# A recurrent two-layer block on one core: negated row maxima transposed twelve columns at a time and sent as one transfer, a turn without TensorE's self-wait, GpSimd's second remainders after the first maxima

## What is computed

```python
    Q, K, V = (heads(WQ), heads(WK), heads(WV))
    score = jnp.einsum('bhqd,bhkd->bhqk', Q, K) / jnp.sqrt(jnp.asarray(D_K, x.dtype))
    score = score + mask
    score = score - jnp.max(score, axis=-1, keepdims=True)
    score = jnp.exp(score)
    score = score / jnp.sum(score, axis=-1, keepdims=True)
    out = jnp.einsum('bhqk,bhkd->bhqd', score, V)
```

```python
    xn = _layernorm(x, axis=-1)
    s = _L0_attn_ref(xn, ...)
    g = _silu(_L0_ffn_ref(xn, ...))
    x = x + s * g
```

## Time and profile before

| | us |
|---|---|
| median of 3 runs | 636.89 (636.42 to 638.6) |
| the profiled execution: its span | 632.9 |
| its own time as a run | not given; the median is 4.0 above the span |
| PE busy | 580.1 (92%) |
| DVE busy | 486.8 (77%) |
| ACT busy | 327.5 (52%) |
| GpSimd busy | 177.4 (28%) |
| chain that ended last | PE 71%, DVE 17%, ACT 3%, issue 3% |

### The profile page before, as it was taken

The page is one execution under the profiler, slowest core; times in us unless marked ns, Lnnn a source line. Parts: engine busy times, 40 slices in busy tenths (PEclk is TensorE's granted clock), DMA queues, the critical chain, the costliest instruction groups (busy, mean ns, idle before and its releaser), DMA issues.

```text
span 632.9 us, 12434 instructions
## 1 busy us (share of the span) xinstructions
PE 580.1 (92%) x4195; PEld 362.5 (57%) x4222; DVE 486.8 (77%) x1174; ACT 327.5 (52%) x587; POOL 177.4 (28%) x162
## 2 busy tenths in 40 slices
PE   2877999999999999899999988888989999999996
PEld 1434544444444445699999963435436666566554
DVE  6789989999989898555555578765779899976465
ACT  2842467575767667555555558664141652263224
POOL 2450000000134342033333320000005687588500
PEclk9888899999999999999999999998799999999999
DMA  7935726060714080221111124205000322331232
GB/s 190 252 119 200 240 69 209 2 207 4 189 53 108 32 239 19 46 53 46 46 50 46 30 79 140 69 14 171 0 13 34 72 66 74 92 110 41 75 100 66
DMA packets 55755, 58.00 MB, mean 92 GB/s; under 512 B 8794, under 2 KB 39546, under 8 KB 55658
## 3 DMA queue, kind: packets, MB, share of 16 engines
q1 hardware_dynamic: 51386, 50.56, 28.4%
q0 software_dynamic: 4320, 6.81, 3.4%
HBM read 41.96 MB, written 18.85 MB: 96 GB/s over the span
## 4 chain that ended last, share of the span: by engine, by line
PE 71%; DVE 17%; ACT 3%; issue 3%; DMA 1%; POOL 1%; SPq 1%; another core or an unknown queue 0%; DVEq 0%; ACTq 0%; PEldq 0%; POOLq 0%
PE banks L1635 11%; PE banks L1780 8%; PE banks L1723 7%; PE banks L1701 7%; PE banks L1912 7%; PE banks L1647 6%; PE banks L1901 5%; PE banks L1898 4%; PE banks L1963 4%; DVE banks L1185 3%; DVE mpart L1188 2%; PE banks L1595 2%; PE banks L1704 2%; ACT arena L754 1%; POOL rows_a L572 1%
## 5 line engine op out<-in xcount | busy, mean ns | idle before, releaser
L754 ACT ACTIVATE arena<-banks 128x512 f32<-128x512 f32 (+1 forms) x304 | 156.3, 585 | 95.5 <-PE banks L1704 53.8
L1723 PE MATMUL banks<-arena 96*128 96x512 bf16 (+3 forms) x384 | 118.3, 339 | 6.0 <-DVE mpart L1185 2.1
L1701 PE MATMUL banks<-arena 128*128 128x512 bf16 (+3 forms) x358 | 106.1, 326 | 5.8 <-ACT arena L754 3.0
L1188 DVE TENSOR_REDUCE mpart<-banks 128x1 f32<-128x512 f32 x128 | 86.1, 685 | 9.4 <-PE banks L1723 8.8
L1185 DVE CUSTOM_DVE_ANT_0 banks<-banks,arena 128x512 f32<-128x512 f32 (+1 forms) x128 | 79.1, 636 | 8.2 <-PE banks L1723 5.3
L1635 PE MATMUL banks<-arena 128*128 128x128 f32 x624 | 76.3, 275 | 1.0 <-ACT arena L695 1.0
L1635 PEld LDWEIGHTS banks<-arena 128*128 128x128 f32 x624 | 72.8, 192 | 1.5 <-ACT arena L695 1.5
L1780 PE MATMUL banks<-arena 128*9 128x512 f32 (+3 forms) x768 | 70.7, 487 | 0.0
L1701 PEld LDWEIGHTS banks<-arena 128*128 128x128 bf16 x384 | 37.8, 99 | 52.3 <-issue 25.6
L797 ACT ACTIVATE arena<-banks 125x512 f32<-125x512 f32 (+2 forms) x48 | 28.5, 595 | 71.3 <-PE banks L1898 46.3
L601 POOL DMA_INDIRECT results<-arena x39 | 37.5, 961 | 88.5 <-DVE arena L1079 88.5
(11 more groups left out here) (293 smaller groups left out, 909.8 us busy)
## 6 DMA issues: line engine op xcount, KB each, us to landing
k_parts<-arena SPq DMA_DIRECT2D x6, 768.0 KB, 7.6
arena<-in_L_ffn_experts_w_dram SPq DMA_DIRECT2D x2, 2048.0 KB, 10.5
arena<-results SPq DMA_DIRECT2D x8, 512.0 KB, 7.3
arena<-k_parts SPq DMA_DIRECT2D x7, 576.0 KB
arena<-q_parts SPq DMA_DIRECT2D x28, 144.0 KB
arena<-in_L_ffn_w_kernel_dram SPq DMA_DIRECT2D x8, 344.0 KB
slots<-in_pad_rows_dram SPq DMA_DIRECT2D x1, 2535.0 KB, 12.2
arena<-slots SPq DMA_DIRECT2D x39, 65.0 KB, 1.9
```

Source lines behind the costliest of these rows:

```text
L754: act.activation(Pr[:, r % 4, heads[0]:heads[-1] + 1, 0:n], ring_e[e % 3][:, 0:len(heads) * n].rearrange("p (j c) -> p j c", j=len(heads)) ...
L1188: ins = dve.tensor_reduce(part, ps[:, 0:n], AX_X, ALU.max)
L1701: ins = pe.matmul(ring_e[e % 3][:, at * n:at * n + n], QK[:, slot, j, 1, P * kt:P * kt + P], QK[:, slot, j, 0, q:q + n], start=True, stop= ...
L1723: ins = pe.matmul(ps[:, at * n:at * n + n], QK[0:TALL, slot, j, 0, P * i:P * i + P], QK[0:TALL, slot, j, 1, 512 * half:512 * half + n], st ...
```

## The change

Three things.

1. MP becomes [slot, 8 tiles, 12 columns], column a x 4 + j for part a of head j, without a memset. A maxima row is four matmuls (one a tile) of 12 stationary columns into partitions 0 to 11; DVE copies only those 12 partitions; SP sends them in one transfer. DVE no longer waits for its own copy nor counts m_free for a maxima row: PE, when it wants that bank again, waits for mrow_ready instead. Tables worked out from PLANS (ring_tables) say which semaphore and value frees each unit.
2. The last transpose of a turn adds to m_ready itself; PE doesn't wait for it. The semaphore turned goes, and ACT waits for m_ready in its place.
3. GpSimd's second pair of remainders (s = 2 and 3) waits for mp_ready, the first negated maxima.

```diff
+def ring_tables():
+    frees, unit_of, reads_before, reads = [], {}, {}, 0
+    for k in range(-1, NG + 1):
+        for step in PLANS[k]:
+            if step[0] in RING_STEPS:
+                unit_of[step] = len(frees)
+            if step[0] == "maxrow":
+                frees.append(("mrow_ready", 2 * step[1] + step[2] + 1))
+            elif step[0] in RING_STEPS:
+                reads += 1
+                frees.append(("m_free", reads))
+            elif step[0] in ("negmax", "experts0"):
+                reads_before[step] = reads
+    return frees, unit_of, reads_before, reads
...
-        MP = region(24832, 1024, BF16).rearrange("p (s m c) -> p s m c", s=2, m=32)
+        MP = region(24832, 2 * QT * 3 * HG // 2, BF16).rearrange("p (s i c) -> p s i c", s=2, i=QT)
...
-                    for j in range(HG):
-                        sp.dma_start(QK[TALL:TALL + 3, g % 3, j, 0, 512 * half:512 * half + 512],
-                                     mrow[32 * j:32 * j + 3, g % 2, 512 * half:512 * half + 512]).then_inc(mrow_in[half], 16)
+                    sp.dma_start(QK[TALL:TALL + 3, g % 3, :, 0, 512 * half:512 * half + 512],
+                                 mrow[0:3 * HG, g % 2, 512 * half:512 * half + 512]).then_inc(mrow_in[half], 16)
...
-            pool.memset(MP, 0.0).then_inc(Z["mem_set"], 1)
...
             for s in (0, 2):
+                if s == 2:
+                    pool.wait_ge(Z["mp_ready"], 1)
                 second_part(s)
...
                         if g >= 1:
-                            act.wait_ge(Z["turned"], 2 * (g - 1) + half + 1)
+                            act.wait_ge(Z["m_ready"], UNIT_OF[("turn", g - 1, half)] + 1)
...
-                        mp = MP[:, g % 2, :, :].rearrange("p (j i) c -> p j i c", j=HG)[:, :, tiles, :]
+                        mp = MP[:, g % 2, tiles, :].rearrange("p i (a j) -> p j i a", j=HG)
...
-                            dve.wait_ge(mrow_in[half], 64 * (g - 1))
-                        dve.tensor_copy(mrow[:, g % 2, 512 * half:512 * half + 512], ps).then_inc(Z["mrow_ready"], 1)
-                        dve.wait_ge(Z["mrow_ready"], 2 * g + half + 1)
-                        dve.sem_inc(Z["m_free"], 1)
+                            dve.wait_ge(mrow_in[half], 16 * (g - 1))
+                        dve.tensor_copy(mrow[0:3 * HG, g % 2, 512 * half:512 * half + 512], ps[0:3 * HG, :]).then_inc(Z["mrow_ready"], 1)
...
             def unit_free():
                 if unit >= 4:
-                    pe.wait_ge(Z["m_free"], unit - 3)
+                    name, n = FREES[unit - 4]
+                    pe.wait_ge(Z[name], n)
...
                         for i in range(4):
-                            for j in range(HG):
-                                ins = pe.matmul(ps[32 * j:32 * j + 32, P * i:P * i + P],
-                                                MP[:, g % 2, j * QT + 4 * half + i, :], ident_b, start=True, stop=True)
+                            ins = pe.matmul(ps[0:3 * HG, P * i:P * i + P], MP[:, g % 2, 4 * half + i, :], ident_b, start=True, stop=True)
...
-                        ins.then_inc(Z["turned"], 1)
-                        pe.wait_ge(Z["turned"], 2 * g + half + 1)
-                        pe.sem_inc(Z["m_ready"], 1)
+                        ins.then_inc(Z["m_ready"], 1)
```

More of the change, by code:

```diff
@@ L210 @@
 PLANS = all_plans()
+RING_STEPS = ("p1", "logits", "counts", "maxrow", "turn", "attn_turn", "attn_out", "x_turn", "places1", "logits1")
+def ring_tables():
[12 more added lines that the diff above has]
+    return frees, unit_of, reads_before, reads
+FREES, UNIT_OF, READS_BEFORE, READS = ring_tables()
 def build(nc, x, WQ, WK, WV, WO, gate, w1, w2, w3, WomT, b_om, log_scale, gamma, beta, W1T, b1, W2T, b2,
@@ L345, in build @@
             p1_done rem_done v_ps v_sb ld_gate lg_ps lg_sb selb_ready pre_ps pre_sb routed
-            m_ready m_free e_ready e_free pv_done o_evac turned mp_ready mrow_ready
+            m_ready m_free e_ready e_free pv_done o_evac mp_ready mrow_ready
             aT_ps aT_sb s_ps rows_ready scattered blkpos_ready a_ps a_sb g_ps u_ps
@@ L1168, in _ @@
             unit = 0
-            dve.wait_ge(Z["mem_set"], 2)
+            dve.wait_ge(Z["mem_set"], 1)
             def unit_ready():
@@ L1211, in _ @@
                         tiles = slice(4 * half, 4 * half + 4)
-                        mp = MP[:, g % 2, :, :].rearrange("p (j i) c -> p j i c", j=HG)[:, :, tiles, :]
+                        mp = MP[:, g % 2, tiles, :].rearrange("p i (a j) -> p j i a", j=HG)
                         top, low = (msm[:, i, :].rearrange("p (j i) -> p j i", j=HG)[:, :, tiles] for i in range(2))
-                        dve.wait_ge(Z["m_free"], unit)
+                        dve.wait_ge(Z["m_free"], READS_BEFORE[step])
                         link(dve.tensor_reduce(top, mpart[:, :, :].rearrange("p (j i) h -> p j i h", j=HG)[:, :, tiles, :], AX_X, ALU.max))
@@ L1233, in _ @@
                         ps = unit_ready().rearrange("p (n j c) -> p n j c", n=4, j=HG)
-                        dve.wait_ge(Z["m_free"], unit)
+                        dve.wait_ge(Z["m_free"], FREES[unit][1] - 1)
                         link(dve.reciprocal(rc[:, :, :], ps[:, :, :, DK]))
@@ L1256, in _ @@
                         if step[1] == 0:
-                            dve.wait_ge(Z["m_free"], unit)
+                            dve.wait_ge(Z["m_free"], FREES[unit - 1][1])
                             dve.wait_ge(Z["ld_posr"], 16)
@@ L1612, in _ @@
             pe.wait_ge(Z["bc_done"], 1)
-            pe.wait_ge(Z["mem_set"], 2)
             pe.wait_ge(Z["sel_d"], 2 * HG - 1)
@@ L1696, in _ @@
                         if kt == 0 and heads[0] == 0:
-                            pe.wait_ge(mrow_in[half], 64 * (k + 1))
+                            pe.wait_ge(mrow_in[half], 16 * (k + 1))
                         if e >= 3:
@@ L1795, in _ @@
                         pe.wait_ge(Z["e_free"], e)
-                        pe.wait_ge(Z["m_free"], unit)
+                        pe.wait_ge(Z["m_free"], READS_BEFORE[step])
+                        pe.wait_ge(Z["mrow_ready"], sum(name == "mrow_ready" for name, _ in FREES[:unit]))
                         experts0()
@@ L1833, in _ @@
                         unit += 1
-            pe.wait_ge(Z["m_free"], unit)
+            pe.wait_ge(Z["m_free"], READS)
             for c in range(2, 4):
```

## The result

Four runs of the changed kernel have a median of 629.29 us (628.88 to 630.05), beside 637.49 us for the kernel before on the same chip: a ratio of 0.9876, 95% interval 0.9861 to 0.9891, 8.2 us less. The forecast was 628.5, within 625.5 to 632.7. The total and the direction came as forecast; the inside did not in every term.

The account below looks back on a forecast made before the run. PE was taken to bound settled head groups and DVE the early ones; 1.95 + 3.4 + 1.6 + 0.2 + 1.2 = 8.35 us off 636.89 gave 628.5 us, range 625.5 to 632.7.

Parts of the forecast that it names:

- Second remainders: Opening: GpSimd's second pair holds three small DVE instructions; delaying it saves 1.95 us, counted whole as in the chain.
- Turns: Attention turns: dropping PE's self-wait saves 0.3 us at each of 11 turns and 0.1 at the last, 3.4.
- DVE's self-wait: After a maxima-row copy: DVE no longer waits for itself, 0.18 us at nine of 16 rows, 1.6.
- Matmuls of a row: Maxima rows: four 12-column matmuls replace 16 of 32 columns, 0.05 us on four rows that count, 0.2.
- full-array form: Maxima rows: if 12 columns ran in full-array mode, about 0.2 us more per row, some 1 us in all.
- Experts' entry: Start of the experts: one transfer for four lets the first block be issued earlier, gain 1.2 us.
- 0.1 to 0.2 until PE goes: Experts' first block: DVE decides at 256.6, and PE starts its turn 0.1 to 0.2 us later.
- The clock: Rival, 15%: PE's 1.2 GHz stretch after a maxima wait vanishes (626.8) or grows to 10 us, costing 3.3 (631.8).
- Landing late: Rival, 7%: in the opening the larger transfer lands at 6.8 us and PE stands; 2 us lost, 630.5.
- DVE taking over: Rival, 18%: DVE or ScalarE becomes the bound, taking back half the turns' and rows' gain, 2.6 us; 631.1.
- rows one after another: Rival, 3%: a maxima row's four narrow matmuls run serially, 1.2 us a row against 0.34; 639.5, slower.
- The 4.0 around the span: Whole run: the median stood 4.0 us above the profiled span, an offset the forecast kept.

Follow-up runs that it names:

- e4: The changed kernel, but GpSimd's second remainders don't wait for the first negated maxima; 632.66 us.
- e11: The kernel before with only GpSimd's wait for the first negated maxima added; 637.58 us, ratio 0.9964.
- e2: The changed kernel, but TensorE again waits for its own transposes in each turn; 633.03 us.
- e10: The changed kernel, but VectorE again waits for its own copy of a maxima row; 632.47 us.
- e5: The changed kernel with maxima-row weights 128 columns wide instead of 12, the other 116 zeros; 628.27 us, ratio 0.9831.
- e3: The changed kernel, but SyncE again sends a maxima row as four transfers of three rows each; 633.68 us.
- e8: The changed kernel, with TensorE reading the first block's expert before its waits for VectorE; 626.61 us, ratio 0.9818.
- e6: The changed kernel with unread matmuls filling TensorE's waits ahead of the first group's two maxima rows; 626.97 us, ratio 0.9823.

## Why the prediction was right, and where not

*Second remainders, 1.95.* The local size is shown in both directions (1.98 in e4, 1.94 in e11), and ScalarE's casts, the store and DVE's row cast came off as forecast. The step that failed in the profiles is "it stands in the chain, so it counts whole". The chain of an execution says what ended last at the clock of that execution. At the first turn 1.1 (e4) and 0.22 (e11) are left, with PE's low stretch longer or differently placed behind it. What the mean over runs keeps isn't shown: 2.3 us by e11's median (0.1 to 4.4), nothing by e4's.

*Turns, 3.4.* After a turn 0.31 less, as forecast (0.3), and 0.1 at the last (1.33 from its first transpose to PE's next matmul instead of 1.43); 2.4 for the others by e2, so about 8 and not 11 of them count. The group shows 0.57 for its two, so in settled groups nearly all count. It is outside them that the count was high: turns 2 to 5 are worth 0.22 together, and the three between the first block and the last turn 0.35.

*DVE's self-wait, 1.6.* The wait alone is worth 0.10 each and 1.1 in e10. Of the group's 0.88 the turns are 0.57, DVE's wait 0.12 and the row 0.02; 0.17 has no experiment of its own. It may come from the second semaphore that the old copy raised, or from turns and copies helping each other; this was not tried. Over the whole first-to-twelfth stretch, 4.2, e2 accounts for 2.0 and e10 for 1.0; 1.2 has no experiment.

*Matmuls of a row, 0.2.* Forecast 0.05 each, got 0.02. The 0.2 a row that the forecast put beside it for the full-array form is there to be had, but the change didn't take it; e5 did.

*Experts' entry, 1.2.* This term was mis-sized: 0.57, of which 0.3 are the transfers (e3). The rest is how the block landed in the first profile: e3 and e11 issue four transfers too, and have entries of 4.38 and 4.34 where the earlier trace rows give 4.65. The failed step is "0.1 to 0.2 until PE goes". PE started 0.70 after DVE, held by the register load, with two waits, that stood behind its wait for DVE (e8). In the kernel before this was hidden: the block's landing came later still, 1.28 after DVE. And the turn's saving, counted in the 3.4, gives nothing here: e2's entry is 4.09.

*The clock* was put as a rival at 15% with a price of 3.3 for a stretch of 10 us. In the first profile it grew from 3.4 to 6.8. It should have been a term of the sum: all three profiles of the changed kernel have it, with 20.4 us from the second negated maxima to the first turn where the kernel before has 19.12, 1.3 more; without any stretch at 1.2 GHz it is 18.21 (e6).

*Landing late, DVE taking over, rows one after another.* One transfer of 12 rows kept nobody waiting, and SP spends 0.8 us on the issue instead of 2.7; how long it took to land no row shows. The rule of the Trainium skill, "DMA: Bandwidth & Descriptors", on why a DMA increments its semaphore by 16, from which four rows one after another on three engines would follow, is therefore neither confirmed nor refuted here. DVE didn't take over in the settled groups, where PE keeps 29.10 of 29.47; that turns 2 to 5 gave next to nothing fits DVE as the bound of the early groups, which wasn't tested. A row stays at 0.32, so its four matmuls don't go one after another.

*The 4.0 around the span.* The changed execution has 1.84 around its span, and those of the later runs 1.8. So the profiled execution before was itself probably some 2 us under the median of 636.89. Keeping the offset was harmless, since it stands on both sides.

By stretches the touched parts give 7.0 where the sum said 8.35; the medians give 8.2, 6.3 and 8.5 on three chips. The forecast's total is thus better than its terms, and that it came within 0.8 us is partly luck: three terms were too large (turns, entry, DVE's wait), the remainders counted whole though half or more went into the clock in the profiles, 1.2 us came from what no term and no experiment names, and the run-to-run spread of start and end covers the 1.3 us between.

## What to carry to other kernels

A wait that is taken away ahead of an engine at its low clock can be partly given back: price it at the next stretch where that engine is the bound, not where the wait stood, and try filling the wait. Of a stall with several causes, list every link with its lateness (block 1.28, register 0.70, DVE 0.16) before giving the whole gap to the last one. And when start and end wander by more than the parts to be measured, cut traces at the same instructions and compare stretches.

## What the runs showed of the hardware that I had not expected

- Matmuls with 12 columns of weights take 0.32 for four and 0.09 from the one before; with 128 columns, 116 of them zeros, 0.23 and nothing. Wider was cheaper in the settled groups.
- Loading one register on TensorE's queue, behind two waits that were already met, costs 0.54 us (0.70 less 0.16) where it stands last.
- Waits of PE of 1.30 and 1.38 us ahead of the first two maxima rows (42.51 and 60.28) were each followed by 1.2 GHz; with both filled (0.20 and 0.15 left in e6) the first low stretch came all the same and the second did not, which took 2.2 us off the way to the first turn.
- One late copy of VectorE near the end (at 583 us) waits up to 4.7 us longer in some executions than PE's matmuls for it need, with a "remote" releaser: in all eight profiles on two of the chips, in none of the six others. What it is stays open; no run here changed it.
